# A wavelet block on one core: channel maxima turned by VectorE, sums kept as rows, and a part of the residual added by engines

## The chip, the cores and the metric

One core of one Trainium2 chip. The metric is device time in microseconds (us) of one launch, median of several runs.

## The reference

x is (8, 256, 160, 160) in float32: 8 images of 256 channels. Weights are small.

```python
wav = concat(haar_dwt(x))                      # 4*256 channels, 80 x 80
fused = relu(bn1(conv1x1(wav, fusion_w, fusion_b)))       # 256 channels
sp_in = concat([mean(fused, channels), max(fused, channels)])
spatial_out = sigmoid(conv7x7(sp_in, sa_w)) * fused
ch_map = sigmoid(mlp(mean(spatial_out, hw)) + mlp(max(spatial_out, hw)))
projected = relu(bn2(conv1x1(ch_map * spatial_out, proj_w, proj_b)))  # 4*256
return haar_idwt(projected) + x
```

So `proj` of an image can start only when the channel gates of the whole image are known, and these only when its 80 x 80 map of channel means and maxima is complete.

## The kernel before, in words

Channels lie on 128 partitions in 2 halves (`i` or `o`). An image is cut into 14 tiles of rows (`ROWS`, line 15: 6 rows of 80 pixels, or 5), so 112 tiles in all; a tile of 6 rows has 480 pixels and 1,920 values of x for each channel half. The program is software pipelined in *slots* (`Slot`, line 21): slot `k` computes `fused` of tile `k` (the *fusion*) and projects tile `kc = k - LAG`, with `LAG = 14 + EXTRA = 20`. So the first 20 slots only fuse (the fill), the next 92 do both (the main phase), and the last 20 only project (the tail). The slot's `phase` is its place in the image that follows the one whose map is being finished: phase 0 ends the convolution, phases 1 to 4 multiply the image by the gates of space in 8 chunks (`GATED`, line 214), and phase 6 (`LAST`) has the channel gates. Each engine has one program and runs it in the order written; semaphores join them.

- **TensorE** (`body`, line 415): `fusion(s, 0)`, `project(s, 0)`, `turn`, `fusion(s, 1)`, `project(s, 1)`. A fusion or a projection of one half is 24 matmuls of 128x128 weights with the tile's pixels (L389, L375; float32 as a high and a low part in three products). `turn` (L410, L412) transposes the row maxima `mx` and multiplies `sm` by ones, row by row, so that both maps lie with columns on partitions in the PSUM tile `pm`. The 7x7 convolution is 14 matmuls (L443).
- **VectorE** (`body`, line 698): `x_lower` (L615, low part of x), `butterflies` (L645, L647, PSUM and `relu` to `sd`), `cells` (L659, `sd` to the output tile), `spatial` (L693, L695, from `turn`'s PSUM to `maps`), `lower` (L676, `y_lo`), `gate` (L669), `channel_max` (L684).
- **ScalarE**: `x_upper` (L463), `relus` (L492), `upper` (L509), `fused` (L536), `chunk_means` (L501).
- **GpSimd** (POOL): `channel_sum` (L314) and `add_x` (L321), a DMA that adds x from DRAM onto the output tile in SBUF. There are 4 output buffers `xout`.
- **SyncE** (SP): the loads of x (L254), the stores (L259, which wait for `x_added`), and the round trip of the space gate through DRAM (L270, L263).

Two places of the code say what sets the order around the change:

```python
for r in range(rows):                       # turn, on TensorE
    pe.transpose(pm[0:W2, r * P:(r + 1) * P], mx[:, r * W2:(r + 1) * W2], ident[:, :])
for r in range(rows):
    mm = pe.matmul(pm[0:W2, MEANS + r:MEANS + r + 1], sm[:, r * W2:(r + 1) * W2],
                   ones[:, 0:1], start=True, stop=True)
```

## Time and profile before

| what | value |
|---|---|
| median of 3 runs | 2601.07 us (2600.91 to 2601.85) |
| the profiled execution | 2597.0 us, span 2595.1 us |
| TensorE busy | 2469.7 us, 95% |
| VectorE busy | 1994.8 us, 77% |
| ScalarE busy | 1077.9 us, 42% |
| GpSimd busy | 355.2 us, 14% |
| DMA | 659.91 MB, 254 GB/s over the span |

A page's busy time is the union of an engine's instructions. "Idle before" says how long an engine stood still ahead of a group and what ended that. An average over the whole span mixes the fill, the main phase and the tail, so the stretches have to be read apart.

### The profile page before, as it was taken

What the parts mean: (1) busy time and instruction counts of PE and PEld (TensorE: products, weight loads), DVE (VectorE), ACT (ScalarE), POOL (GpSimd) and SP (SyncE); (2) the same over time, 40 slices, a digit from 0 to 9 for tenths busy, and PEclk for the clock granted to TensorE, in tenths of its full rate; (3) what the DMA queues carried; (4) which work ended last, traced back from release to release, by engine and by line L of the source; (5) the groups of instructions that cost most, each with busy time, mean ns of one, the idle gap of its engine ahead of it and who ended that gap; (6) DMA issues with size and microseconds to landing.
All of it is one profiled execution on the core that took longest, in us unless ns stands there. A gap on an engine that the chain in (4) does not pass through costs nothing. (4 is left out here: it accounts for less than half of the span.)

```text
span 2595.1 us, 32968 instructions
## 1 busy us (share of the span) xinstructions
PE 2469.7 (95%) x12996; PEld 2200.7 (85%) x12996; DVE 1994.8 (77%) x2560; ACT 1077.9 (42%) x1413; POOL 355.2 (14%) x346
## 2 busy tenths in 40 slices
PE   4999999999999999999999999999999999987874
PEld 3888889898898989989898988989899898976764
DVE  4656777798778887798777987788877987787875
ACT  2445534354344533354434543345333453334221
POOL 0100111111111111111111111111111111111110
PEclk9999999999999999999999999999999999998897
DMA  3445699999999999999999999999999999898999
GB/s 125 157 147 195 185 267 262 257 297 270 256 270 273 287 261 260 250 304 271 265 266 256 303 263 261 262 280 286 260 259 263 295 268 267 242 248 237 277 272 245
DMA packets 115178, 659.91 MB, mean 254 GB/s; under 512 B 19520, under 2 KB 20560, under 8 KB 115024
## 3 DMA queue, kind: packets, MB, share of 16 engines
q1 hardware_dynamic: 82768, 448.07, 48.8%
q0 software_dynamic: 32256, 209.73, 41.6%
q8 instruction: 103, 1.69, 0.2%
q14 instruction: 51, 0.42, 0.0%
HBM read 447.83 MB, written 209.92 MB: 253 GB/s over the span
## 5 line engine op out<-in xcount | busy, mean ns | idle before, releaser
L375 PE MATMUL pp<-y_hi,wp_hi 128*128 128x480 f32 (+1 forms) x1792 | 674.5, 376 | 59.1 <-DVE y_lo L676 35.8
L615 DVE TENSOR_TENSOR x_lo<-xin,x_hi 128x1920 fp32r<-128x1920 f32 (+1 forms) x224 | 474.0, 2116 | 302.3 <-ACT x_hi L463 302.2
L389 PE MATMUL pf<-x_hi,wf_hi 128*128 128x480 f32 (+1 forms) x1792 | 676.4, 377 | 6.5 <-ACT fused L536 3.5
L375 PE MATMUL pp<-y_lo,wp_hi 128*128 128x480 f32 (+1 forms) x1792 | 670.6, 374 | 0.0
L375 PE MATMUL pp<-y_hi,wp_lo 128*128 128x480 f32 (+1 forms) x1792 | 669.0, 373 | 0.0
L389 PE MATMUL pf<-x_lo,wf_hi 128*128 128x480 f32 (+1 forms) x1792 | 664.5, 371 | 0.0
L389 PE MATMUL pf<-x_hi,wf_lo 128*128 128x480 f32 (+1 forms) x1792 | 664.3, 371 | 0.0
L463 ACT ACTIVATE x_hi<-xin 128x1920 fp32r<-128x1920 f32 (+1 forms) x224 | 418.5, 1869 | 572.1 <-PE pf L389 572.1
L659 DVE SCALAR_TENSOR_TENSOR xout<-sd,both 128x960 f32<-128x960 f32 (+1 forms) x448 | 504.8, 1169 | 49.2 <-DMA out_dram<-xout 41.9
L492 ACT ACTIVATE relu<-pp,t 128x480 f32<-128x480 f32 (+1 forms) x448 | 286.3, 642 | 390.4 <-PE pp L375 349.0
L375 PEld LDWEIGHTS pp<-y_hi,wp_hi 128*128 128x128 f32 x1792 | 341.9, 191 | 110.0 <-DVE y_lo L676 40.6
L321 POOL DMA_DIRECT2D xout<-in_x_dram x224 | 196.7, 878 | 1679.7 <-DVE xout L659 1679.7
L389 PEld LDWEIGHTS pf<-x_hi,wf_hi 128*128 128x128 f32 x1792 | 337.1, 188 | 51.0 <-issue 13.2
L375 PEld LDWEIGHTS pp<-y_hi,wp_lo 128*128 128x128 f32 x1792 | 341.5, 191 | 41.2
L375 PEld LDWEIGHTS pp<-y_lo,wp_hi 128*128 128x128 f32 x1792 | 341.2, 190 | 38.6
L389 PEld LDWEIGHTS pf<-x_lo,wf_hi 128*128 128x128 f32 x1792 | 336.9, 188 | 39.5
L389 PEld LDWEIGHTS pf<-x_hi,wf_lo 128*128 128x128 f32 x1792 | 337.4, 188 | 36.4
L645 DVE SCALAR_TENSOR_TENSOR sd<-pp,nbias,relu 128x480 f32<-128x480 f32 (+1 forms) x448 | 306.6, 684 | 22.2 <-PE pp L375 19.9
L536 ACT ACTIVATE fused<-pf,t 128x480 f32<-128x480 f32 (+1 forms) x224 | 141.0, 643 | 400.3 <-PE pf L389 400.2
L647 DVE SCALAR_TENSOR_TENSOR sd<-pp,nbias,relu 128x480 f32<-128x480 f32 (+1 forms) x448 | 305.7, 682 | 0.0
L314 POOL TENSOR_TENSOR sm<-fused 128x480 f32<-128x480 f32 (+1 forms) x112 | 159.4, 1423 | 545.0 <-DVE mx L684 261.5
L669 DVE CUSTOM_DVE_ANT_0 fused<-fused,sigb 128x800 f32<-128x800 f32 x128 | 121.7, 988 | 54.1 <-DMA sigb<-sig_scratch 54.1
(82 smaller groups left out, 1117.2 us busy)
## 6 DMA issues: line engine op xcount, KB each, us to landing
xin<-in_x_dram SPq DMA_DIRECT2D x160, 960.0 KB, 8.3
xout<-in_x_dram POOLq DMA_DIRECT2D x160, 960.0 KB, 10.9
out_dram<-xout SPq DMA_DIRECT2D x160, 960.0 KB, 11.8
xin<-in_x_dram SPq DMA_DIRECT2D x64, 800.0 KB, 7.5
xout<-in_x_dram POOLq DMA_DIRECT2D x64, 800.0 KB, 10.7
out_dram<-xout SPq DMA_DIRECT2D x64, 800.0 KB, 11.0
sigb<-sig_scratch SPq DMA_DIRECT2D x64, 400.0 KB, 8.1
fused<-in_L_conv_fusion_w_dram SPq DMA_DIRECT2D x1, 1024.0 KB, 4.9
```

What stands on the lines that cost most here:

```text
L314: nc.gpsimd.tensor_tensor(sm[:, 0:n], fused[:, 0, ring(s.k)], fused[:, 1, ring(s.k)], ALU.add).then_inc(sm_ready, 1)
L321: nc.gpsimd.dma_start(xout[:, g % 4, 0:4 * px_of(kc)], dram(x_v, kc, i), accum_op=ALU.add).then_inc(x_added[g % 4], 16)
L375: mm = pe.matmul(pp[j][:, 0:n_px], w[:, kt, cols], y[:, s.pc, kt, 0:n_px], start=(kt == 0 and m == 0), stop=(kt == CT - 1 and m == 2))
L389: mm = pe.matmul(pf[o][:, 0:n_px].rearrange("p (y w) -> p y w", w=W2), w[:, i, q, o * P:(o + 1) * P], v[:, q % 2, :, q // 2, :], start=(i ...
L463: nc.scalar.activation(halves(x_hi, i, k), pairs(i, k), ACT.Copy).then_inc(xhi_ready[i], 1)
L492: nc.scalar.activation(relu[:, n, 0:n_px], pp[j][:, 0:n_px], ACT.Relu, bias=bias2[:, j * CT + i:j * CT + i + 1]).then_inc(r_ready, 1)
L536: nc.scalar.activation(fused[:, o, ring(s.k)], pf[o][:, 0:px_of(s.k)], ACT.Relu, bias=bias1[:, o:o + 1]).then_inc(f_ready, 1)
L615: nc.vector.tensor_tensor(halves(x_lo, i, k), pairs(i, k), halves(x_hi, i, k).bitcast(F32), ALU.subtract).then_inc(xlo_ready[i], 1)
L645: nc.vector.scalar_tensor_tensor(rows[:, :, 0, :], p, low, q, ALU.max, ALU.add).then_inc(sd_ready, 1)
L647: nc.vector.scalar_tensor_tensor(rows[:, :, 1, :], p, low, q, ALU.max, ALU.subtract).then_inc(sd_ready, 1)
L659: nc.vector.scalar_tensor_tensor(px[:, :, :, c], s0, both[:, c, i:i + 1], s1, ALU.add, op).then_inc(cell_ready, 1)
L669: nc.vector.tensor_tensor_reduce(f, f, sigb[:, :], 1.0, 0.0, ALU.mult, ALU.max, part[:, 1, i, c:c + 1]).then_inc(mult_done, 1)
```

## The change

Five things are changed.

1. `turn` is gone. VectorE turns `mx` in blocks of 32x32 (`turn`, now on VectorE) and takes the maximum over each block into `blockmax`; once per image TensorE transposes `blockmax` (2 transposes into `across`), VectorE takes the maxima over the 4 partition groups, and SyncE sends the map through DRAM to lay it as rows. `mx` and `turned` lie in `sd`.
2. The channel sums are gathered by rows in PSUM: one matmul per row, with `pick` as weights, which puts the sum of row `at` into PSUM row `at` of a group of 32; ScalarE scales the finished map once per image.
3. `EXTRA` is 7, so `LAG` is 21; the convolution moves from phase 0 to phase 1, `GATED` to phases 2 to 5, `LAST` is 7.
4. x is added by DMA only for half `i = 1` of a tile, and only while `kc + LAG < NT` (not in the tail). Otherwise x is loaded by SyncE into `xre`, the projection's result goes to `cell`, and VectorE adds one half of the pixels and GpSimd the other (`residual`). There are 3 buffers `xre` where there were 4 `xout`.
5. GpSimd's additions wait for VectorE's `x_lower`.

```diff
-EXTRA = 6
+EXTRA = 7
-        xout = sb("xout", [P, 4, XPM])
+        xre = sb("xre", [P, 3, XPM])
-        mx = sb("mx", [P, PXM])
+        cell = sb("cell", [P, XPM])
+        mx = sd[:, 0, 0:PXM]
+        turned = sd[:, 1, 0:PXM]
-        GATED = {1: (0, 1), 2: (2, 3), 3: (4, 5), 4: (6, 7)}
+        GATED = {2: (0, 1), 3: (2, 3), 4: (4, 5), 5: (6, 7)}
+        def adding(kc, i):
+            return i == 1 and kc + LAG < NT
+        def residual(eng, ops, kc, i, hand, added):
+            g = 2 * kc + i
+            n = 2 * px_of(kc)
+            part_of = slice(hand * n, (hand + 1) * n)
+            eng.wait_ge(xre_landed[g % 3], 16 * uses(g, False))
+            eng.wait_ge(cell_ready, 2 * (g + 1))
+            x_part = xre[:, g % 3, part_of]
+            ops.tensor_tensor(x_part, x_part, cell[:, part_of], ALU.add).then_inc(added, 1)
...
             def body(s):                                   # SyncE
+                if s.phase in GATED:
+                    load_sig(s, GATED[s.phase][0])
+                if s.load_second:
+                    load_x(s.k + 2, 0)
+                if s.c and not s.c_is_first:
+                    store(s.kc - 1, 1)
+                if s.c and not adding(s.kc, 1):
+                    load_residual(s.kc, 1)
+                if s.phase in GATED:
+                    load_sig(s, GATED[s.phase][1])
+                if s.load_second:
+                    load_x(s.k + 2, 1)
+                if s.phase == 0:
+                    sp.wait_ge(maxima_ready, s.nb + 1)
+                    sp.dma_start(map_dram.rearrange("o (h p j) -> (o p) h j", h=2, j=GROUP), maxima[:, :, :]
+                                 ).then_inc(map_stored, 16)
...
+                if s.c:
+                    store(s.kc, 0)
+                if s.c_next:
+                    load_residual(s.kn, 0)
+                if s.phase == 0:
+                    sp.wait_ge(map_stored, 16 * (s.nb + 1))
+                    need(sp, conv_psum, s.nb)
+                    sp.dma_start(maps[:, 1, PAD:PAD + W2], map_dram.rearrange("o (h w) -> (o h) w", w=W2)
+                                 ).then_inc(map_landed, 16)
...
             def body(s):                                   # GpSimd
+                if s.c and not s.c_is_first:
+                    if adding(s.kc - 1, 1):
+                        add_x(s.kc - 1, 1)
+                    else:
+                        residual(gp, nc.gpsimd, s.kc - 1, 1, 1, added_p)
+                if s.turn:
+                    channel_sum(s)
                 if s.c:
-                    add_x(s.kc, 1)
+                    if s.load_next:
+                        gp.wait_ge(xlo_ready[1], s.k + 2)
+                    elif s.c_next and not s.next_is_first:
+                        gp.wait_ge(lo_ready, CT * (s.kn + 1))
+                    residual(gp, nc.gpsimd, s.kc, 0, 1, added_p)
...
+            def add_channels(s):                           # TensorE
+                k = s.k - 1
+                pe.wait_ge(sm_ready, k + 1)
+                for r in range(ROWS[k % TILES]):
+                    row = FIRST[k % TILES] + r
+                    at, base = row % GROUP, row - row % GROUP
+                    m = min(GROUP, H2 - base)
+                    mm = pe.matmul(sums[base:base + m, :], pick[:, GROUP - 1 - at:GROUP - 1 - at + m],
+                                   sm[:, r * W2:(r + 1) * W2], start=(at == 0), stop=(at == m - 1))
...
+                if s.phase == 1:
+                    pe.wait_ge(mean_ready, s.nb + 1)
+                    pe.wait_ge(map_landed, 16 * (s.nb + 1))
...
+            def turn(s):                                   # VectorE
+                nc.vector.transpose(turned[:, 0:blocks * GROUP], mx[:, 0:blocks * GROUP]).then_inc(turned_ready, 1)
+                nc.vector.tensor_reduce(blockmax[:, block:block + blocks],
+                                        turned[:, 0:blocks * GROUP].rearrange("p (n c) -> p n c", c=GROUP),
+                                        AX.X, ALU.max).then_inc(blockmax_ready, 1)
...
                 if s.c:
                     butterflies(s, 1)
+                    residual(dve, nc.vector, s.kc, 0, 0, added_v)
                     cells(s, 1)
```

**Three places of the order.** TensorE around a turn of the second image, before: L375 is the end of `project(s, 0)`, L410 and L412 are `turn`, L389 begins `fusion(s, 1)`.

```order
L375 MATMUL pp<-y_hi,wp_hi 128x480
L375 MATMUL pp<-y_hi,wp_lo 128x480
L375 MATMUL pp<-y_lo,wp_hi 128x480
L410 MATMUL pm<-ident,mx 80x128 x6
L412 MATMUL pm<-ones,sm 80x1 x6
L389 MATMUL pf<-x_hi,wf_hi 128x480
```

With the change, in phase 1 of the same image: L467 is the end of `fusion(s, 1)`, L486 is `add_channels`, L517 the convolution, L453 begins `project(s, 1)`.

```order
L467 MATMUL pf<-x_hi,wf_hi 128x480
L467 MATMUL pf<-x_hi,wf_lo 128x480
L467 MATMUL pf<-x_lo,wf_hi 128x480
L486 MATMUL pm<-sm,pick 32x80 x6
L517 MATMUL pm<-maps,band 80x80 x14
L453 MATMUL pp<-y_hi,wp_hi 128x480
```

The six transposes of a slot are gone, the six sums have 80 moving columns where they had one, they stand behind both fusions, and the convolution stands in the slot of phase 1 where it closed that of phase 0.

VectorE in a slot of the main phase with the change (L733 and L735 are the butterflies, L753 the cells, L786 the channel maximum, L698 `x_lower`):

```order
L770 SCALAR_TENSOR_TENSOR y_lo<-fused,ch,y_hi 128x480 x2
L786 TENSOR_TENSOR sd<-fused 128x480
L698 TENSOR_TENSOR x_lo<-xin,x_hi 128x1920
L795 STREAM_TRANSPOSE sd<-sd 128x480
L798 TENSOR_REDUCE blockmax<-sd 128x15
L733 SCALAR_TENSOR_TENSOR sd<-pp,nbias,relu 128x6x80
```

The transpose and the reduction stand between `x_lower` and the second butterflies; `spatial`'s two instructions, which stood ahead of `y_lo`, are gone.

SyncE around the end of an image with the change (L296 loads x, L304 loads the residual, L313 stores):

```order
L296 DMA xin<-in_x_dram 128x1920
L337 DMA map_scratch<-maxima 100x2x32
L313 DMA out_dram<-xre 128x1920
L304 DMA xre<-in_x_dram 128x1920
L351 DMA maps<-map_scratch 80x80
L296 DMA xin<-in_x_dram 128x1920
L313 DMA out_dram<-xre 128x1920
L296 DMA xin<-in_x_dram 128x1920
L342 DMA sig_scratch<-sig 80x80
```

The rows of L337 and L351 are new: a store and a load of the map of maxima, with one store and one load of a tile between them.

## Rows read from the trace of the kernel before

**Rows 1.** Windows: main phase, tail to LAST, rest of tail; busy by engine, PEclk, DMA share.
```profile
330.00:2200.00 1870.00, 1870.00 (x9959) 1676.89 (x9958) 1502.86 (x1848) 816.24 (x1070) 277.94 (x258) 1.00 0.97 270
...
2283.40:2379.50 96.10, 69.82 (x322) 59.34 (x320) 78.29 (x119) 36.51 (x70) 11.01 (x13) 0.88 0.98 261
2379.50:2595.10 215.60, 155.36 (x672) 132.63 (x672) 149.04 (x196) 51.43 (x84) 24.72 (x29) 0.88 0.97 255
```

**Rows 2.** Line 516, ScalarE's gate of space, in two successive images.
```profile
L516 ACT ACTIVATE sig<-pm x1: 234/234/234, 784.8 to 784.8; 80x80 f32<-80x80 f32 x1
...
L516 ACT ACTIVATE sig<-pm x1: 234/234/234, 1088.6 to 1088.6; 80x80 f32<-80x80 f32 x1
```

**Rows 3.** Timeline of PE around one turn: start us, us, engine, line.
```profile
641.68 0.38 PE L375 MATMUL pp<-y_hi,wp_lo 128*128 128x480 f32 x1
...
642.77 0.82 PE L410 MATMUL pm<-ident,mx 128*80 128x128 f32 x6
643.42 0.95 PE L412 MATMUL pm<-ones,sm 128*80 128x1 f32 x12
644.24 0.46 PE L389 MATMUL pf<-x_hi,wf_hi 128*128 128x480 f32 x1
644.54 0.38 PE L389 MATMUL pf<-x_hi,wf_lo 128*128 128x480 f32 x1
```

**Rows 4.** Timeline of PE around one convolution.
```profile
478.78 2.17 PE L443 MATMUL pm<-band,maps 80*80 80x80 f32 x28
480.74 0.46 PE L389 MATMUL pf<-x_hi,wf_hi 128*128 128x480 f32 x1
```

**Rows 5.** Timeline of DVE, a slot without gates.
```profile
641.82 0.71 DVE L645 SCALAR_TENSOR_TENSOR sd<-pp,nbias,relu 128x480 f32<-128x480 f32 x1
...
644.44 2.35 DVE L659 SCALAR_TENSOR_TENSOR xout<-sd,both 128x960 f32<-128x960 f32 x2
646.71 0.94 DVE L693 TENSOR_REDUCE maps<-pm 80x6 f32<-80x768 f32 x1
...
647.64 1.33 DVE L676 SCALAR_TENSOR_TENSOR y_lo<-fused,ch,y_hi 128x480 fp32r<-128x480 f32 x2
```

**Rows 6.** Timeline of DVE, slots with gates.
```profile
499.24 0.99 DVE L669 CUSTOM_DVE_ANT_0 fused<-fused,sigb 128x800 f32<-128x800 f32 x1 [1.72 <-DMA sigb<-sig_scratch]
...
501.07 0.66 DVE L684 TENSOR_TENSOR mx<-fused 128x480 f32<-128x480 f32 x1
501.64 2.15 DVE L615 TENSOR_TENSOR x_lo<-xin,x_hi 128x1920 fp32r<-128x1920 f32 x1
...
523.90 3.13 DVE L615 TENSOR_TENSOR x_lo<-xin,x_hi 128x1920 fp32r<-128x1920 f32 x1 [0.24 <-ACT x_hi L463]
```

**Rows 7.** Timeline of POOL in the same slots.
```profile
501.87 3.01 POOL L314 TENSOR_TENSOR sm<-fused 128x480 f32<-128x480 f32 x1 [5.28 <-issue]
...
523.79 1.22 POOL L314 TENSOR_TENSOR sm<-fused 128x480 f32<-128x480 f32 x1 [3.49 <-issue]
```

**Rows 8.** The page, DMA queues (packets, MB, share) and issues (KB, us to landing).
```profile
q1 hardware_dynamic: 82768, 448.07, 48.8%
q0 software_dynamic: 32256, 209.73, 41.6%
...
sigb<-sig_scratch SPq DMA_DIRECT2D x64, 400.0 KB, 8.1
...
sig_scratch<-sig SPq DMA_DIRECT2D x8, 25.0 KB, 13.0
```

**Rows 9.** Timeline of DVE in the tail.
```profile
2385.51 0.72 DVE L645 SCALAR_TENSOR_TENSOR sd<-pp,nbias,relu 128x480 f32<-128x480 f32 x1 [4.62 <-PE pp L375]
...
2403.03 1.34 DVE L676 SCALAR_TENSOR_TENSOR y_lo<-fused,ch,y_hi 128x480 fp32r<-128x480 f32 x2
...
2414.28 1.34 DVE L676 SCALAR_TENSOR_TENSOR y_lo<-fused,ch,y_hi 128x480 fp32r<-128x480 f32 x2
```

**Rows 10.** Waits of DVE in the tail: us in total, times, longest.
```profile
DVE xout L659 <- DMA out_dram<-xout: 41.9, 20, 4.9
```

More of the change, by code:

```diff
@@ L289, in _ @@
                 body(s)
-            for i in range(CT):
-                store(NT - 1, i)
-            for p in range(4):
-                sp.wait_ge(stored[p], 16 * len(range(p, 2 * NT, 4)))
+            store(NT - 1, 1)
+            for p in range(3):
+                sp.wait_ge(stored[p], 16 * len(range(p, 2 * NT, 3)))
         @block.gpsimd
@@ L429, in body @@
-                if s.c:
+                elif s.c:
                     pe.wait_ge(lo_ready, CT * (s.kc + 1))
                     project(s, 0)
-                if s.phase != LAST:
-                    if s.turn:
-                        turn(s)
-                    if s.a:
-                        fusion(s, 1)
+                if s.a:
+                    fusion(s, 1)
+                if s.turn:
+                    add_channels(s)
+                if s.phase == 0:
+                    pe.wait_ge(blockmax_ready, s.k)
+                    for h in range(2):
+                        n = NPX // GROUP // 2
+                        mm = pe.transpose(across[:, h * P:(h + 1) * P], blockmax[:, h * n:(h + 1) * n], ident[:, :])
+                    mm.then_inc(across_psum, 1)
@@ new lines, in body @@
+                if s.phase == 1:
+                    pe.wait_ge(mean_ready, s.nb + 1)
+                    pe.wait_ge(map_landed, 16 * (s.nb + 1))
+                    pe.wait_ge(band_pass, KS * NK)
+                    for j in range(NK):
+                        mm = pe.matmul(conv, band[:, j, :], maps[:, j // KS, j % KS:j % KS + W2],
+                                       start=(j == 0), stop=(j == NK - 1))
+                    mm.then_inc(conv_psum, 1)
+                if s.phase == LAST:
+                    pe.wait_ge(lo_ready, CT * (s.kc + 1))
+                    project(s, 0)
@@ L533, in body @@
                 if s.a:
+                    if s.phase == LAST and s.c:
+                        act.wait_ge(lo_ready, CT * (s.kc + 1))
                     for o in range(CT):
@@ L636, in butterflies @@
                 n_px = px_of(s.kc)
+                if s.a and (i == 1 or s.phase == LAST):
+                    dve.wait_ge(turned_ready, s.k + 1)
+                    dve.wait_ge(blockmax_ready, s.k + 1)
                 for n, j in enumerate((LL, HL)):
@@ L707, in body @@
                     lower(s.kc)
-                if s.c and not ahead:
+                elif s.c:
                     butterflies(s, 0)
+                    if not s.c_is_first and not adding(s.kc - 1, 1):
+                        residual(dve, nc.vector, s.kc - 1, 1, 0, added_v)
                     cells(s, 0)
-                if s.turn and not ahead:
-                    spatial(s)
                 if s.c_next and not s.next_is_first and not ahead:
@@ L719, in body @@
                     nc.vector.tensor_reduce(pool[:, :, 1], part[:, 1, :, :], AX.X, ALU.max).then_inc(pool_ready, 1)
-                if ahead and s.turn:
-                    spatial(s)
                 if s.phase in GATED:
@@ L727, in body @@
                     x_lower(s.k + 1, 1)
+                if s.a:
+                    turn(s)
+                if s.phase == 0:
+                    spatial_max(s)
                 if ahead:
```

207 lines of the change are left out of this document (112 added, 95 removed).

## The prediction

> **What bounds the kernel now.** I read the windows first, by stage. In the main phase (330 to 2200 us) TensorE is busy for all of 1870.00 us at a granted clock of 1.00, VectorE for 1502.86 us (80%), and the DMA engines for 0.97 of the time [rows 1]. The reader should see that nothing there ever stops TensorE; whatever shortens its own work shortens the main phase, and nothing else does. The period confirms it: the space gate of one image stands at 784.8 us and that of the next at 1088.6 [rows 2], 303.8 us apart. The tail is another matter. From its start at 2283.4 to the y_lo of LAST it takes 96.1 us, and from there to the end, for 14 tiles, 215.6 us; TensorE is busy in only 72% of either part at a mean clock of 0.88, while the DMA share stays at 0.97 to 0.98 [rows 1]. VectorE waits there 20 times, 41.9 us in all, for a store to free an output buffer [rows 10]. So the tail is bound by transfers: per byte the DMA that adds costs 41.6/209.73, against 48.8/448.07 for plain ones, 1.8 times as much [rows 8].
>
> **The change, part by part**, against the profiled execution's 2597.0 us.
>
> *TensorE's map work.* Before, one turn of six rows goes from 642.77 to 644.24, 1.47 us, and the first matmul behind it takes 0.30 us to the next one instead of 0.22 (642.77 less 641.68 is five steps of 0.218) [rows 3]: 1.55 us. Five rows by the same rates: 1.31. With the change a row is one float32 matmul of 80 moving columns. Its nearest row is the convolution, 14 matmuls in 1.96 us [rows 4], so 0.14 us each; six make 0.84, with the same 0.08 behind them 0.92 us, five 0.78. Saved: 0.63 and 0.53 us. An image has ten tiles of six rows and four of five, 8.4 us, and eight images 67 us. The new `across` transposes, 2 a image at the old transposes' 0.11 and 0.08 behind them, cost 0.3 us, 2 us in all. **-65 us.** Bounds: 0.11 us a row (the transposes, 0.65/6 [rows 3]) and 0.245 (a whole row of the old turn, 1.47/6) give -84 and 0. I take the convolution's price since shape and type agree.
>
> *VectorE in the main phase.* Gone: the reduction and scaling, from 646.71 to 647.64, 0.93 us [rows 5]. New in a slot of six rows: the addition of 960 elements, half an x_lower of 1920 (2.15 us [rows 6]), 1.07; a transpose of 480 elements and a reduction to 15 columns. Neither is in the trace. For each I take the step of the channel maximum over the same 480 elements, 0.57 us (501.07 to 501.64 [rows 6]); bounds are half of that and the old reduction's 0.94 [rows 5]. Net +1.28 us a slot. VectorE's busy time per image is 1502.86/1870 of 303.8, 244 us, and becomes about 261 of 295: 88%. The fullest slots are those with gates: two x_lower 4.3, eight butterflies 5.2 (four from 641.82 to 644.44), four cells 4.5 (two from 644.44 to 646.71 [rows 5]), y_lo 1.3, maximum 0.57, four gate halves 3.7 (two from 499.24 to 501.07 [rows 6]), and the new 2.2: 21.8 us. TensorE's slot is 96 steps of 0.218 and 0.92, 21.9 us. That fits by a hair, between slots with 3.7 us to spare. I cost it at nothing: TensorE covers it, and if that cover is gone each us of excess is a us of the slot.
>
> *The map's round trip.* In phase 0 VectorE's maxima over the groups come behind its transpose and reduction, by the order of the program about 22 us into the slot; the convolution stands some 17 us into the next slot of 22, 17 us later. Between lie a small store, whose like takes 13.0 us to land, and a small load, with 8.1 us for the load of the gates [rows 8]: 21.1 and some 0.7 us of issue, against 17. With half of the adding DMAs gone the engines' share falls from 0.97 to about 0.86 (the software queue's 41.6% of engine time halves, and plain loads take up 0.55 of that half), so I take 18.9 us in place of 21.8: a wait of 2 us in each of the 7 images of the main phase, **+15 us**. Bounds: 0 and 5 us each, 0 and 35. Behind SyncE's wait for the first of these stand the second and then the next slot's x; x of that slot waits for an x_lower that is not done earlier anyway. What is late next is the gate load of phase 2, a slot later than before, so it has the same room as now.
>
> *The longer lag.* One slot of the main phase becomes a slot of the fill: 48 steps of 0.218 less, **-10.5 us**; the tail gets it back below.
>
> *The tail.* The adding DMAs go, and a tile needs 3.93 MB of plain transfer. At 448.07 MB in 48.8% of 2595 us (354 GB/s [rows 8]) that is 11.1 us, and TensorE's 48 steps are 10.5. VectorE takes over: with no wait it went from one y_lo at 2403.03 to the next at 2414.28 in 11.25 us [rows 9], and two additions of 1.07 make 13.4 (11.2 with five rows). From LAST's y_lo to the end: 6 us until the first butterflies (to 2385.51 [rows 9]), ten tiles of 13.4 and four of 11.2 for 179 us, and 9 us for the last addition (GpSimd's 960 elements twice its 1.22 [rows 7]) and a store of 6 us: 194, against 215.6, -22 us. Ahead of LAST there are now seven slots for six: two of 13.4, a stall of 6 for the map's round trip, which nothing covers there, three of 13.4 + 3.7 + 0.5 with gates, one such of five rows 15.4, and 14.2 for the last: 115 against 96.1, +19 us. **-3 us.** Bounds: the present 215.6/14 = 15.4 us a tile gives +22 instead of -22 in the second part, a wait-free TensorE's 10.5 gives -50.
>
> *Everything else* goes together at 0: 2 small copies by ScalarE per image, the loads at the start, the convolution's own 14 matmuls.
>
> Sum: 2597.0 - 65 + 15 - 10.5 - 3 = 2533.5 us. The runs' median, 2601.07, lies 4.1 us above the profiled 2597.0, so I forecast **2538 us**, 2.4% less.
>
> **GpSimd beside VectorE.** The trace shows that these two hinder each other. GpSimd's sum that began at 501.87, while VectorE was in the x_lower of 501.64, took 3.01 us instead of 1.22, and the x_lower that began at 523.90, 0.11 us after GpSimd's sum, took 3.13 instead of 2.15 [rows 6, 7]. Each lost about what was left of the other's instruction. The change adds GpSimd 960 elements a slot, 2.4 us, twice that in the tail, but makes it wait for x_lower, behind which VectorE has a transpose, a reduction and butterflies with one operand in PSUM. In the main phase that is 0.57 + 0.57 + 2.6 = 3.7 us of cover for 2.4 us, so the sum has nothing for it. The Trainium skill (SBUF — State Buffer, "Who interferes with whom") says that a VectorE instruction with two SBUF inputs and a GpSimd instruction that reads SBUF take one shared port, that whichever starts first keeps it for its whole length, and that one with a single SBUF input is free of it. By that rule the trace agrees, and the sum stands as long as the two stay apart; where they meet, its time is the last rival's.
>
> **The rivals.**
>
> *The round trip holds TensorE up.* If both transfers take as long as now or longer (queued behind a tile's store and load, about 9 us of wait), 7 x 9 replaces 15: 2586 us. For: 13.0 and 8.1 are the rows. Against: less DMA work.
>
> *The tail stays bound by transfers.* Three buffers for four, each held for a load, an addition and a store; if a tile takes 15.4 us as now, the second part costs 216 in place of 194 and the first some 10 more: 2570 us. For: a share of 0.97. Against: 11.1 us of transfer per 13.4.
>
> *Better than forecast.* The sums cost 0.11 us a row, the map arrives in time, the additions run beside waits: 2538 - 17 - 15 = 2506 us.
>
> *Slower than before: GpSimd meets VectorE.* Place: the main phase, where GpSimd has 1.2 + 2.4 us a slot. If these fall on two-input instructions, VectorE's gated slots take 21.8 + 3.6 = 25.4 against 21.9: 3.5 us for four slots of an image, 7 images, 98 us, so 2538 + 98 = 2636 us. It decides once more than 2.3 us of the 3.6 fall so in every gated slot. Against: the new waits, with 3.7 us of cover. For: VectorE has no time to spare there.
>
> **How the numbers follow.** Forecast 0.50, round trip 0.14, tail 0.13, better 0.14, GpSimd 0.09. The time is the forecast's. The range takes in the better case, the tail and the round trip with the forecast's own bounds, 2503 to 2594, and leaves out GpSimd's case and the ends. A measurement of this kernel can tell about 0.2%, 5 us, from no change. Only the last case is slower; between it and the others little is left: faster 0.88, same 0.03, slower 0.09.
>
> **What would show it.** TensorE 100% busy in the main phase with images 296 us apart plus the wait; a turn of six sums near 0.92 us; a wait of TensorE on the map's DMA near 2 us once an image; VectorE near 88%; additions of 960 at 1.07 us on VectorE and 2.4 on GpSimd; tail tiles of 13.4 us with VectorE without waits. The forecast is wrong if TensorE waits for VectorE in the gated slots, if x_lower or cells get longer on average, or if VectorE waits for stores or for `xre` in the tail.

## The result, and the profile after

| | before | changed |
|---|---|---|
| median | 2600.99 us | 2618.7 us (2616.93 to 2620.59, 4 runs) |
| profiled execution, span | 2597.0, 2595.1 us | 2619.5, 2617.7 us |
| ratio to before | | 1.0072, 95% interval 1.0054 to 1.0089 |

The change makes the kernel 0.7% slower. I forecast 2538 us in 2503 to 2594, so the time is outside the range and its sign is wrong. The channel gates (ScalarE's sigmoid into `ch`, line 524 before and 596 now) cut a run into comparable stretches; the same table serves for the experiments.

| stretch | before | changed | difference |
|---|---|---|---|
| start to the first channel gates | 291.4 | 299.4 | +8.0 |
| six images of the main phase, each | 303.8 | 307.2 | +3.4, six times +20.5 |
| the last image to its gates | 264.3 | 279.3 | +15.0 |
| from there to the end | 216.5 | 195.6 | -20.9 |

The transfers changed as intended. The adding DMAs are down from 209.73 MB at 41.6% of engine time to two fifths of that [rows 8]:

```profile
q1 hardware_dynamic: 104368, 573.01, 61.2%
q0 software_dynamic: 13104, 85.20, 16.8%
...
xin<-in_x_dram SPq DMA_DIRECT2D x160, 960.0 KB, 6.4
...
xre<-in_x_dram POOLq DMA_DIRECT2D x65, 960.0 KB, 11.4
...
sigb<-sig_scratch SPq DMA_DIRECT2D x64, 400.0 KB, 5.3
```

The gates' own load lands in 5.3 us at the median where it took 8.1. But that median mixes two: in 330 to 2200 us the first gate's load of a slot takes 10.1 us at the median, where it took 8.6, and the second one's 4.7, where it took 8.2. The windows of [rows 1] now read:

```profile
core 0: us, PE busy (x) PEld busy (x) DVE busy (x) ACT busy (x) POOL busy (x), PEclk, DMA share, GB/s
330.00:2200.00 1870.00, 1831.62 (x9390) 1607.09 (x9390) 1596.13 (x1922) 812.18 (x1070) 362.39 (x255) 0.99 0.85 268
2283.40:2379.50 96.10, 70.34 (x294) 57.72 (x292) 83.11 (x99) 27.49 (x49) 26.32 (x11) 0.83 0.69 234
2379.50:2595.10 215.60, 167.59 (x724) 141.71 (x725) 202.41 (x258) 63.08 (x108) 65.58 (x30) 0.92 0.74 262
```

The first row is where the kernel loses. TensorE, never idle there before, now stands still for 1870.00 - 1831.62 = 38.4 us, though VectorE is busy for only 1596.13 us, 85%. Who stops TensorE, in the waits of the same window:

```profile
PE pm L486 <- POOL sm L384: 23.0, 13, 2.9
PE pp L453 <- DVE sd L735: 14.0, 10, 2.4
```

Two releasers: GpSimd's channel sum (`sm`) and VectorE's butterflies (`sd`). Neither is the map's round trip, which costs nothing in this window. The wait for `sd` goes back to a VectorE that is late in slots with gates. Of the 23.0 us for `sm`, six waits of 2.9 us lie elsewhere, in the slot of the channel gates. VectorE's timeline from the first gate of one slot (gate A; its second is gate B) to gate A of the next slot:

```profile
860.74 0.99 DVE L763 CUSTOM_DVE_ANT_0 fused<-fused,sigb 128x800 f32<-128x800 f32 x1 [2.70 <-DMA sigb<-sig_scratch]
...
864.87 0.67 DVE L795 STREAM_TRANSPOSE sd<-sd 128x480 f32<-128x480 f32 x1
865.58 0.65 DVE L798 TENSOR_REDUCE blockmax<-sd 128x15 f32<-128x480 f32 x1
866.32 0.72 DVE L733 SCALAR_TENSOR_TENSOR sd<-pp,nbias,relu 128x480 f32<-128x480 f32 x1
...
868.83 1.15 DVE L271 TENSOR_TENSOR xre<-xre,cell 128x960 f32<-128x960 f32 x1
...
872.16 0.98 DVE L763 CUSTOM_DVE_ANT_0 fused<-fused,sigb 128x800 f32<-128x800 f32 x1
...
873.98 1.82 DVE L698 TENSOR_TENSOR x_lo<-xin,x_hi 128x1600 fp32r<-128x1600 f32 x1
...
884.59 0.99 DVE L763 CUSTOM_DVE_ANT_0 fused<-fused,sigb 128x800 f32<-128x800 f32 x1 [3.48 <-DMA sigb<-sig_scratch]
```

From 860.74 to 884.59 are 23.85 us, of which VectorE waits 3.48 for `sigb`. In between it has no other gap, so its work is 20.4 us, in a slot that is partly of tiles of five rows; in the fullest slots, with six rows throughout, it is 22.0, for the 21.8 of the prediction. The work is as the sum said, and it is the wait ahead of the gate that doesn't fit. That wait isn't new: in 330 to 2200 us VectorE waited as long in all for these loads before, in shorter pieces (first line before, second changed; total, times, longest):

```profile
DVE fused L669 <- DMA sigb<-sig_scratch: 40.6, 31, 2.4
DVE fused L763 <- DMA sigb<-sig_scratch: 41.3, 19, 3.5
```

New are the longer single waits and a slot without slack to take them up. The reader should find the cause in SyncE's queue and GpSimd's timeline of that slot:

```profile
870.01 0.34 SPq L313 DMA_DIRECT2D out_dram<-xre  x1
870.39 0.43 SPq L304 DMA_DIRECT2D xre<-in_x_dram  x1
874.09 0.32 SPq L319 DMA_DIRECT2D sigb<-sig_scratch  x1
```

```profile
865.04 2.27 POOL L271 TENSOR_TENSOR xre<-xre,cell 128x960 f32<-128x960 f32 x1 [11.61 <-DVE x_lo L698]
872.60 0.88 POOL L391 DMA_DIRECT2D xre<-in_x_dram  x1 [5.29 <-DVE xre L753]
875.95 1.19 POOL L384 TENSOR_TENSOR sm<-fused 128x480 f32<-128x480 f32 x1 [2.47 <-issue]
```

The gate's load is issued at 874.09, once the gate before it is done with the one buffer, behind a store of 960 KB (870.01), the new load of x (870.39, 800 KB) and the adding DMA (872.60). It lands at 884.6, in 10.5 us. And the sum of 875.95 begins when VectorE's x_lower (873.98, behind gate B) is over, because the change makes it wait for that: point 5 of the change names this wait for the additions alone, but the channel sum has it too (`xlo_ready[0]`), where it waited for `mx_ready` before. TensorE then stands still:

```profile
877.18 1.02 PE L486 MATMUL pm<-sm,pick 128*32 128x80 f32 x12 [1.53 <-POOL sm L384]
...
891.19 0.46 PE L453 MATMUL pp<-y_hi,wp_hi 128*128 128x400 f32 x1 [2.40 <-DVE sd L735]
892.05 0.54 PE L453 MATMUL pp<-y_hi,wp_lo 128*128 128x400 f32 x1
...
901.82 0.34 PE L453 MATMUL pp<-y_hi,wp_hi 128*128 128x400 f32 x1
...
920.35 0.88 PE L486 MATMUL pm<-sm,pick 128*32 128x80 f32 x10 [2.92 <-POOL sm L384]
```

The longest wait, 2.92 us, is in the slot of the channel gates. Behind the wait of 2.40 us the same matmul takes 0.54 instead of 0.34 us until 895.05: the granted clock is at 1.2 GHz for 3.4 us (0.51 in 891.9 to 895.3). Ten steps of 0.33 us instead of 0.18 cost another 1.5.

The turn itself, in the layout of [rows 3]:

```profile
948.43 0.38 PE L467 MATMUL pf<-x_lo,wf_hi 128*128 128x480 f32 x1
948.74 1.02 PE L486 MATMUL pm<-sm,pick 128*32 128x80 f32 x12
949.68 0.48 PE L453 MATMUL pp<-y_hi,wp_hi 128*128 128x480 f32 x1
950.00 0.38 PE L453 MATMUL pp<-y_hi,wp_lo 128*128 128x480 f32 x1
```

From 948.43 to 950.00 are 1.57 us, two steps of 0.218 of which are the fusion's and the projection's own: 1.13 us for six rows, where I had 0.92. The saving is 0.42 us a turn, not 0.63.

In the tail, VectorE and GpSimd ahead of the last channel gates, and TensorE's convolution:

```profile
2334.29 0.99 DVE L763 CUSTOM_DVE_ANT_0 fused<-fused,sigb 128x800 f32<-128x800 f32 x1
...
2335.20 3.01 DVE L763 CUSTOM_DVE_ANT_0 fused<-fused,sigb 128x800 f32<-128x800 f32 x1
...
2338.14 0.70 DVE L733 SCALAR_TENSOR_TENSOR sd<-pp,nbias,relu 128x480 f32<-128x480 f32 x1
```

```profile
2334.45 2.90 POOL L271 TENSOR_TENSOR xre<-xre,cell 128x960 f32<-128x960 f32 x1 [5.15 <-DVE y_lo L770]
```

```profile
2310.97 4.00 PE L517 MATMUL pm<-maps,band 80*80 80x80 f32 x28 [8.12 <-issue]
```

GpSimd's addition starts 0.16 us into the first gate half and takes 2.90 us instead of 2.27, and the second half takes 3.01 us instead of 0.99. That happens in each of the eight gates of this stretch, twice with 2.7, in all 15.5 us. The convolution waits 8.12 us for the map, once, where nothing covers it.

### The profile page after: what moved, and what is told of

Same layout as the page of the kernel before. It is cut to its first block and busy times, and to the rows that moved or that the text cites. A ratio compares the mean times of both kernels' runs of the same rounds, so it can differ in the third digit from the quotient of the medians.

```text
span 2617.7 us, 32607 instructions
## 1 busy us (share of the span) xinstructions
PE 2445.5 (93%) x12372; PEld 2135.2 (82%) x12372; DVE 2180.0 (83%) x2701; ACT 1078.3 (41%) x1421; POOL 513.5 (20%) x347
## 5 line engine op out<-in xcount | busy, mean ns | idle before, releaser
L453 PE MATMUL pp<-y_hi,wp_hi 128*128 128x480 f32 (+1 forms) x1792 | 691.1, 386 | 78.3 <-DVE sd L735 44.7
L453 PE MATMUL pp<-y_lo,wp_hi 128*128 128x480 f32 (+1 forms) x1792 | 675.9, 377 | 0.0
L453 PE MATMUL pp<-y_hi,wp_lo 128*128 128x480 f32 (+1 forms) x1792 | 674.7, 377 | 0.0
L467 PE MATMUL pf<-x_hi,wf_hi 128*128 128x480 f32 (+1 forms) x1792 | 668.4, 373 | 3.8 <-DVE x_lo L698 3.0
L467 PE MATMUL pf<-x_hi,wf_lo 128*128 128x480 f32 (+1 forms) x1792 | 665.3, 371 | 0.0
L467 PE MATMUL pf<-x_lo,wf_hi 128*128 128x480 f32 (+1 forms) x1792 | 664.9, 371 | 0.0
L698 DVE TENSOR_TENSOR x_lo<-xin,x_hi 128x1920 fp32r<-128x1920 f32 (+1 forms) x224 | 461.7, 2062 | 221.6 <-ACT x_hi L539 221.6
L271 POOL TENSOR_TENSOR xre<-xre,cell 128x960 f32<-128x960 f32 (+1 forms) x133 | 297.0, 2233 | 1124.7 <-DVE x_lo L698 806.9
L453 PEld LDWEIGHTS pp<-y_hi,wp_hi 128*128 128x128 f32 x1792 | 345.4, 193 | 143.4 <-DVE sd L735 57.0
L453 PEld LDWEIGHTS pp<-y_hi,wp_lo 128*128 128x128 f32 x1792 | 345.7, 193 | 38.8
L453 PEld LDWEIGHTS pp<-y_lo,wp_hi 128*128 128x128 f32 x1792 | 345.1, 193 | 39.1
L467 PEld LDWEIGHTS pf<-x_hi,wf_hi 128*128 128x128 f32 x1792 | 337.0, 188 | 47.2 <-issue 5.6
L467 PEld LDWEIGHTS pf<-x_hi,wf_lo 128*128 128x128 f32 x1792 | 337.7, 188 | 39.0
L467 PEld LDWEIGHTS pf<-x_lo,wf_hi 128*128 128x128 f32 x1792 | 337.1, 188 | 39.1
L733 DVE SCALAR_TENSOR_TENSOR sd<-pp,nbias,relu 128x480 f32<-128x480 f32 (+1 forms) x448 | 307.9, 687 | 38.2 <-PE pp L453 27.7
L753 DVE SCALAR_TENSOR_TENSOR cell<-sd,both 128x960 f32<-128x960 f32 (+1 forms) x266 | 299.8, 1169 | 9.4 <-POOL xre L271 2.2
L735 DVE SCALAR_TENSOR_TENSOR sd<-pp,nbias,relu 128x480 f32<-128x480 f32 (+1 forms) x448 | 306.4, 684 | 0.0
L384 POOL TENSOR_TENSOR sm<-fused 128x480 f32<-128x480 f32 (+1 forms) x112 | 134.9, 1205 | 486.3 <-DVE x_lo L698 277.5
L753 DVE SCALAR_TENSOR_TENSOR xre<-sd,both 128x960 f32<-128x960 f32 (+1 forms) x182 | 204.6, 1166 | 0.0
```

What stands on the lines that cost most here:

```text
L271: ops.tensor_tensor(x_part, x_part, cell[:, part_of], ALU.add).then_inc(added, 1)
L384: nc.gpsimd.tensor_tensor(sm[:, 0:n], fused[:, 0, ring(k)], fused[:, 1, ring(k)], ALU.add).then_inc(sm_ready, 1)
L453: mm = pe.matmul(pp[j][:, 0:n_px], w[:, kt, cols], y[:, s.pc, kt, 0:n_px], start=(kt == 0 and m == 0), stop=(kt == CT - 1 and m == 2))
L467: mm = pe.matmul(pf[o][:, 0:n_px].rearrange("p (y w) -> p y w", w=W2), w[:, i, q, o * P:(o + 1) * P], v[:, q % 2, :, q // 2, :], start=(i ...
L698: nc.vector.tensor_tensor(halves(x_lo, i, k), pairs(i, k), halves(x_hi, i, k).bitcast(F32), ALU.subtract).then_inc(xlo_ready[i], 1)
L733: nc.vector.scalar_tensor_tensor(rows[:, :, 0, :], p, low, q, ALU.max, ALU.add).then_inc(sd_ready, 1)
```

## The experiments

Three explanations stood after the result. Waits: VectorE is late in the gated slots since the gates' load stands behind the added transfers, and the channel sum stands behind a late x_lower. Contention: GpSimd's additions take VectorE's time. Map: TensorE's part of the change is itself no gain. Twelve kernels were run; an expectation's letters A and B hold for its own run. The stretches in the table come from the profiled executions. The kernel before had medians of 2599.0 to 2599.6 us beside these runs, single ones between 2585 and 2607, so a few us between two rows of the table say nothing unless one stretch holds them. How much a stretch itself varies is seen in e6, e7, e8 and e10, which run the same program until the tail: their images last 302.5, 301.5, 302.1 and 302.8 us, so differences of 1 us an image between rows are not told apart.

| run | median us | ratio, 95% interval | to first gates | each of six images | last image | to the end |
|---|---|---|---|---|---|---|
| before | 2601 | 1 | 291.4 | 303.8 | 264.3 | 216.5 |
| changed | 2618.7 | 1.0072 (1.0054 to 1.0089) | 299.4 | 307.2 | 279.3 | 195.6 |
| e1_all_dma | 2600.6 | 1.0014 (0.9997 to 1.0031) | 300.6 | 302.2 | 262.8 | 220.2 |
| e2_dma_main | 2580.5 | 0.9940 (0.9919 to 0.9961) | 299.9 | 302.4 | 268.4 | 195.5 |
| e3_sum_free | 2625.9 | 1.0120 (1.0085 to 1.0155) | 289.9 | 309.7 | 278.8 | 196.2 |
| e4_sig_first | 2601.8 | 1.0015 (1.0000 to 1.0029) | 300.1 | 304.2 | 278.5 | 196.1 |
| e5_sum_last | 2608.4 | 1.0038 (1.0024 to 1.0051) | 290.8 | 307.0 | 278.6 | 196.3 |
| e6_dma_sum | 2571.3 | 0.9895 (0.9865 to 0.9925) | 290.0 | 302.5 | 269.7 | 195.2 |
| e7_dma_tail | 2559.0 | 0.9857 (0.9826 to 0.9888) | 289.8 | 301.5 | 261.0 | 195.5 |
| e8_quarter | 2567.2 | 0.9882 (0.9852 to 0.9912) | 290.8 | 302.1 | 262.2 | 201.4 |
| e9_two_causes | 2588.1 | 0.9949 (0.9933 to 0.9966) | 289.7 | 303.7 | 278.4 | 196.1 |
| e10_vector_all | 2586.2 | 0.9948 (0.9934 to 0.9963) | 291.1 | 302.8 | 261.8 | 220.2 |
| e11_sums_twice | 2628.9 | 1.0106 (1.0091 to 1.0121) | 303.7 | 310.0 | 265.9 | 194.7 |
| e12_best | 2562.1 | 0.9846 (0.9831 to 0.9861) | 291.1 | 302.2 | 261.0 | 195.6 |

**e1_all_dma.** The map's part of the change alone, with three buffers. Here, in e2 and in all kernels built on them the queue's order in SyncE changes as well, beside the line shown: the store of half 0 comes a slot later, and the store and the load of x for half 1 stand behind the second gate's load:

```diff
-            return i == 1 and kc + LAG < NT
+            return True
```

> The map part of the change alone: x is added by DMA for every half tile, in the tail too; VectorE and GpSimd add nothing. Theory A (VectorE is overfull in the four gated slots, 22.1 us of work and 3 us of waiting for the gates against TensorE's 21.9): without the additions VectorE has 1.1 us less per slot, TensorE's waits of 6.4 us an image go, images are about 299.5 us apart, and the tail is bound by transfers as before, so 2575 to 2600 us. Theory B (GpSimd's channel sum, which now waits for x_lower, is what stops TensorE): that wait is still there, TensorE still waits some 6 us an image, images near 306 us, about 2615 us.

It lies between the two: TensorE's wait for `sd` in 330 to 2200 us falls from 14.0 to 3.5 us, as in A, and 13.4 of the 23.0 us for `sm` stay, as in B. An image lasts 302.2 us, 1.6 less than before where the prediction's turns and `across` gave 8, and the start is 9 us slower. The tail behind the last gates is no shorter than before. So the map's part gains little as it stands, and x by engines in the tail is worth 25 us, from 220.2 to 195.6. Ahead of the last gates it costs: all 16 gate halves of e1's tail take 0.99 us, and from the last gate of space (ScalarE's `sig`) to the last channel gates are 91.2 us, where the changed kernel takes 107.1. The difference, 15.9 us, is that kernel's 15.5 us of slow gates.

**e2_dma_main.** x by DMA for both halves in the main phase, by engines in the tail:

```diff
-            return i == 1 and kc + LAG < NT
+            return kc + LAG < NT
```

> x is added by DMA for both halves outside the tail, by the engines in the tail. Theory A: images 299.5 us apart instead of 307.2, tail as in the changed kernel (195.6 us behind LAST), so 2619 less 7 times 7.7, about 2565 us. Theory B: images near 306 us, about 2610 us. If the two adding DMAs bind again (a share near 0.97), the x loads or stores show up as waits.

2580.5 us, between A and B, and faster than both kernels, by 38 us than the changed one. An image lasts 302.4 us where it lasted 307.2, so the engines' additions in the main phase are what costs there: 4.8 us an image, in spite of a DMA share of 0.96 instead of 0.85 in 330 to 2200 us. It doesn't tell waits from contention: both the loads of `xre` and the additions are gone. The last image gains 11 us too, though the engines add there as before. In its tail only four gate halves are slow (7.7 us) where eight were; the load of x for half 1 now comes later in the queue, but whether that is why wasn't tried.

**e3_sum_free.** The channel sum no longer waits for x_lower:

```diff
-                if s.load_next:
-                    gp.wait_ge(xlo_ready[0], s.k + 2)
```

> GpSimd's channel sum no longer waits for x_lower of the slot, only for fused and for its own PSUM group. Theory B: TensorE's waits on sm (about 4 us an image) go and nothing comes for them, about 2590 us. Theory A: TensorE then waits for VectorE's sd instead, and GpSimd now meets two-input instructions of VectorE, 2605 to 2620 us.

It is slower than theory A's 2620, and shows what that wait buys. The gates on VectorE in 330 to 2200 us, of the changed kernel and of this one:

```profile
L763 DVE CUSTOM_DVE_ANT_0 fused<-fused,sigb 128x800 f32<-128x800 f32 x96 | 91.2, 988 | 41.3 <-DMA sigb<-sig_scratch 41.3
```

```profile
L761 DVE CUSTOM_DVE_ANT_0 fused<-fused,sigb 128x800 f32<-128x800 f32 x96 | 126.2, 1351 | 12.8 <-DMA sigb<-sig_scratch 12.8
```

The mean gate half goes from 988 to 1351 ns, 35 us more work, of which 28.5 are won back as shorter waits for `sigb`; an image lasts 2.5 us longer. But the start is 9.5 us shorter (289.9 for 299.4): where nothing is projected, the wait buys nothing and holds TensorE up 17 times for 0.4 to 1.5 us, 11.8 us in all. That gave e5.

**e4_sig_first.** SyncE issues the next slot's first gate load before the load of x into `xre`:

```diff
                 if s.c:
                     store(s.kc, 0)
+                if s.phase is not None and s.phase + 1 in GATED:
+                    load_sig(s, GATED[s.phase + 1][0])
                 if s.c_next:
                     load_residual(s.kn, 0)
```

> SyncE issues the first gate load of a slot ahead of the load of the residual instead of behind it. Theory A: VectorE's waits for the gates (41 us in the main phase) fall by about half, TensorE's waits with them, 3 us an image, about 2597 us. Theory B: VectorE waits less, TensorE as long as before, 2619 us.

17 us less, near theory A's 2597, with all the additions and bytes in place. The waits of TensorE and, in the second fence, of VectorE in 330 to 2200 us:

```profile
PE pm L486 <- POOL sm L384: 21.0, 12, 2.9
PE pm L528 <- DVE pool L833: 1.7, 6, 0.3
```

```profile
DVE fused L763 <- DMA sigb<-sig_scratch: 8.3, 10, 2.3
```

VectorE's wait for `sigb` falls from 41.3 to 8.3 us, and TensorE's wait for `sd`, 14.0 us before, is gone. The first gate's load now lands in 7.8 us at the median (10.1), the second one's in 6.4 (4.7). That shows the explanation by waits: a queue's order made VectorE late, in slots that its work already fills (e12 tries the same order where it has slack). It gives 3.0 of the 4.8 us an image that e2 gave. The wait for `sm`, 2.9 us in the slot of the channel gates, is untouched.

**e5_sum_last.** The sum waits only where it buys something:

```diff
-                if s.load_next:
+                if s.load_next and s.c and s.phase != LAST:
                     gp.wait_ge(xlo_ready[0], s.k + 2)
```

> The changed kernel, but GpSimd's channel sum waits for the next tile's low halves only in slots that also project and are not the slot of the channel gates; in the first 17 slots and in that one slot of each image it starts as soon as the tile's fused values stand. Theory A (the sum's wait, put there so that it runs beside no VectorE work it would slow, is itself a price: 0.7 us of TensorE in each of the first 17 slots and 2.9 us once an image, with a clock dip behind it): the first channel gates come at 290 instead of 299.4, an image lasts 307.2 less 3 to 4 us, in all 2618.7 - 9.5 - 7 x 3.5 = 2585. Theory B (as when the wait was dropped everywhere, the sum then runs beside VectorE's work and slows it, so that nothing is won in the main phase): the first 9.5 us alone, 2609, or worse.

Theory B's 2609 is met: 10 us, nearly all at the start. In the main phase it gives 0.2 us an image, less than can be told apart. In the slot of the channel gates the sum starts earlier but meets x_lower and y_lo on VectorE and takes 1.95 us where it took 1.37 (906.61 here, 918.93 before), so TensorE still waits 2.3 us for it, for 2.9.

**e6_dma_sum.** e2 and e5 together.

> x by DMA for both halves of each tile in the main phase, engines in the tail, and the channel sum's wait dropped as in the run before. With VectorE unloaded the sum can start early without harm. Theory A: 290 for the first channel gates, an image of 302.4 less 2.2 us of wait less 1.5 us of clock = 299, 268 for the last interval, 195.5 behind it: 2550. Theory B (302.4 an image is what TensorE's work and clock make of it, the sum's wait only stands where another wait would): 290 first, 302.4 an image: 2571.

2571.3, theory B's number; that it fits to the microsecond is luck, its four runs lie between 2566 and 2571.5. The start takes 290.0 us, an image 302.5. TensorE's idle time in 330 to 2200 us didn't fall (17.4 us in e2, 20.1 here): the waits for `sm` got shorter and waits for VectorE came in their place.

**e7_dma_tail.** As e6, with x by DMA up to the last image but one:

```diff
-            return kc + LAG < NT
+            return kc + TILES < NT
```

> As the run before, with x by DMA also for the tiles of the second but last image that are finished in the tail, so that the gates there have no GpSimd work beside them; the engines add x for the last image alone. Theory A (the second gate of each of these slots took 3.0 instead of 1.0 us beside GpSimd's addition, which makes the last interval 268 where it is 263 with x by DMA): 5 us less than the run before. Theory B (that stretch is held by the map's round trip and the butterflies' chain, or with the DMA engines full again it pays what it gains): within 2 us of it.

12 us less than e6, of which 8.7 in the stretch that it changes, more than theory A's 5; the rest lies in images whose program is the same. In e6 four gate halves of that stretch were slow, 7.7 us in all; here none is. A second gate half there, of e2 and of this kernel:

```profile
2322.56 3.01 DVE L769 CUSTOM_DVE_ANT_0 fused<-fused,sigb 128x800 f32<-128x800 f32 x1
```

```profile
2306.17 0.99 DVE L769 CUSTOM_DVE_ANT_0 fused<-fused,sigb 128x800 f32<-128x800 f32 x1
```

So contention is real, and its place is the tail's gates. At 0.9857 of the time before this is, with e12, the fastest version found.

**e8_quarter.** As e7, VectorE adds a quarter of each half tile, GpSimd three quarters:

```diff
-            part_of = slice(hand * n, (hand + 1) * n)
+            part_of = slice(0, 1 * n // 2) if hand == 0 else slice(1 * n // 2, 2 * n)
```

> As the run before, but VectorE adds x to a quarter of each half tile and GpSimd to three quarters (each had a half), for the last image's 14 tiles, behind the last channel gates. That stretch is 195.5 us with VectorE busy 93 per cent. Theory A (VectorE's own work bounds it): each tile saves two times 0.57 us on VectorE, 14 x 1.15 = 16 us less than the run before. Theory B (while GpSimd reads and writes, VectorE's operations of the same kind stand still or nearly so, as y_lo's did, 3.34 against 1.33 us): GpSimd's two additions last 4.5 instead of 3.0 us each and VectorE loses up to that much again: no gain, or up to 20 us slower.

Theory B: the last stretch is 201.4 for 195.5. VectorE's and GpSimd's addition in one half tile:

```profile
2463.95 1.21 DVE L271 TENSOR_TENSOR xre<-xre,cell 128x400 f32<-128x400 f32 x1
```

```profile
2461.94 2.77 POOL L271 TENSOR_TENSOR xre<-xre,cell 128x1200 f32<-128x1200 f32 x1 [3.88 <-DVE y_lo L776]
```

GpSimd's ends at 2464.71, 0.76 us into VectorE's, which takes 1.21 us for half the elements of what took 0.98 in e7: it stands until the other is through, then works 0.45. Four of these additions, with 0.28, 0.63, 0.75 and 0.76 us beside GpSimd's, all end 0.43 to 0.45 us behind it. With a half, GpSimd's 1.92 us end within the four butterflies.

**e10_vector_all.** As e7, VectorE adds all of it in the last image:

```diff
+            if hand:
+                return
...
-            part_of = slice(hand * n, (hand + 1) * n)
+            part_of = slice(0, 2 * n)
```

> As the kernel with x by DMA up to the second but last image (2559), but VectorE adds x to the whole of each half tile and GpSimd to none of it, for the last image's 14 tiles; that stretch is 195.5 us, with VectorE busy 93 per cent. Theory A (VectorE's own work bounds it, and GpSimd's half is a gift): VectorE has two times 1 us more in each tile, 14 x 2 = 28 us slower, 2587. Theory B (GpSimd's half costs VectorE nearly as much as it takes away, as the run with three quarters on GpSimd suggests): under 10 us slower, 2559 to 2569.

Theory A here: 27 us slower, 24.7 of them in that stretch, against 28 expected. GpSimd's half is nearly free where it lies beside butterflies, and a half is the best of the three shares tried.

**e9_two_causes.** The changed kernel with the edits of e4 and e5:

> The changed kernel with both of its causes of lateness taken out that were tried apart: the first gate's load goes ahead of the x load in its queue (alone 17 us), and the channel sum waits for the low halves only in slots that project and are not the channel gates' (alone 10 us). Theory A (two separate causes; the second gained only 1 us in the main phase since the first still stood behind it): 2618.7 - 17 - 10 = 2592, and 2585 if the second now gains in the main phase too, with images of about 302.5. Theory B (they overlap: both paid for the same late VectorE): 2600.

2588.1, faster than before, where e4 and e5 alone give 17 and 10 of the 30.6 us: two causes that add, and a little more, at theory A's figures for the time but not for its images of 302.5. An image lasts 303.7, still 2 more than in e7, and the traces show where. In the slot of the channel gates VectorE's addition of 0.98 us stands ahead of its cells, GpSimd's adding DMA waits for the cells, and the channel sum comes behind it. TensorE around 900 us, in e9 and in e7:

```profile
899.58 1.23 PE L486 MATMUL pm<-sm,pick 128*32 128x80 f32 x10 [2.31 <-POOL sm L384]
```

```profile
895.88 0.88 PE L492 MATMUL pm<-sm,pick 128*32 128x80 f32 x10 [1.51 <-POOL sm L388]
```

The wait is 0.8 us longer, and beside it the granted clock is at 1.2 GHz for 3.4 us in each of e9's six images but in only one of e7's. No run takes this wait away by itself.

**e11_sums_twice.** As e7, each row's sum matmul issued twice:

```diff
+                    for again in range(2):
```

> As the kernel with x by DMA up to the second but last image (2559), but TensorE makes each row's sum matmul twice into the same PSUM rows (the scale behind it is halved, so the result is the same). It prices the turn: a six-row turn now holds TensorE 1.13 us, of which 12 matmuls are 0.95 between their starts. Theory A (TensorE bounds fill and main phase, so what is added to its work is added to the time): 98 tiles in the fill and the main phase that fuse under TensorE's bound, and 14 more, by about 0.9 us each, 2559 + 90 to 100 = 2650 to 2660. Theory B (other engines hold the main phase, TensorE has room): under 50 us more.

Between both: 70 us more, 0.62 a tile. A six-row turn is now 1.77 us between starts, for 0.94:

```profile
1001.78 1.85 PE L493 MATMUL pm<-sm,pick 128*32 128x80 f32 x24
1003.55 0.49 PE L459 MATMUL pp<-y_hi,wp_hi 128*128 128x480 f32 x1
```

So each added row costs 0.14 us, and an image gets some 11.1 us of work (ten turns of 0.83 and four of 0.7) but lasts only 8.5 longer. TensorE is busy for 1768.06 of 1770.00 us from 330 to 2100, where it was busy for 1757.12 in e7: of the missing 2.6 us, 1.9 went into idle time that it filled. TensorE bounds both kernels, with little idle time between.

**e12_best.** e7 with the edit of e4:

> As the kernel with x by DMA up to the second but last image (2559), with the first gate's load ahead of the other loads in the queue as well. In that kernel VectorE waits only some 2.5 us an image for gates and is behind nowhere but around the channel gates. Theory A (a late gate costs only where VectorE has no slack): no gain in the main phase, 1 to 5 us in the last image's gates, 2554 to 2559. Theory B (each microsecond of a gate's wait reaches TensorE): 15 us less, 2544.

No gain, at theory A's edge: the median is 3 us above e7's, and the runs are the same, 2557.03 to 2562.52 us against e7's 2557.07 to 2565.23. A late gate costs only where VectorE has no slack.

## Why the prediction was wrong

My sum is 2533.5, a span of 2531.6; the span came out at 2617.7, 86 us more. By stretches: the terms make an image 303.8 - 8.4 + 0.3 + 2 = 297.7 us, and six images miss by 9.5 each, 57 us; the last stretch misses by 1; 28 us lie at the start and in the last image up to its gates.

- **VectorE in the main phase: the step that failed.** It said that the gated slots' 21.8 us "fits by a hair", and "I cost it at nothing: TensorE covers it". The work was as counted, 22.0 us in the fullest slots: additions of 1.15 (I had 1.07), transpose and reduction in steps of 0.71 and 0.74 (I had 0.57), GpSimd's addition 2.27 (2.4). What the list of the slot's instructions left out is that the gate itself waits for a load. The rows of before show that wait (1.72 us at 499.24 [rows 6]) and VectorE's slack hid it there; the change takes the slack away and puts a load of x in the gate load's way, which makes single waits up to 3.5 us. A slot that "fits by a hair" can't carry that wait: TensorE waited 14.0 us for VectorE's `sd` in the main phase, in place of nothing. e4 shows it: 3.0 us an image, 17 in all. I named SyncE's queue only for the map, and called the gate load "the same room as now".
- **GpSimd's channel sum: left out.** The prediction counted GpSimd's new wait for x_lower as protection and looked only at what it keeps apart. It didn't say who waits for the sum: TensorE. That costs 9 us in the fill (e5). In the main phase TensorE waits for the sum above all once an image, 2.9 us in the slot of the channel gates, and dropping the wait there takes only 0.6 us off it.
- **TensorE's map work: right mechanism, wrong size.** 1.13 us a turn instead of 0.92; a turn of six rows saves 0.42 instead of 0.63, and 112 turns by 0.21 make 24 us, the largest single miss. The rate per row was right (e11: 0.14 us). What I missed is the switch: the first one starts 0.31 us behind the last fusion step instead of 0.22 and the six then take 0.94, not 0.84. My bounds held it.
- **The map's round trip: too dear in the main phase.** I put 2 us into each of seven images (14, entered as 15). It costs none there. The maxima stand 17 us ahead of the convolution, as I had it, but the trip from the store's issue to the load's landing takes 11.8 us (771.55 to 783.3), not 18.9, and the map lies there 3.8 to 5.3 us early in six images:

```profile
771.55 0.32 SPq L337 DMA_DIRECT2D map_scratch<-maxima  x1
776.04 0.85 SPq L351 DMA_DIRECT2D maps<-map_scratch  x1
788.21 2.23 PE L517 MATMUL pm<-maps,band 80*80 80x80 f32 x28
```

  In the tail it costs 8.1 us, where I had 6.
- **The tail's second part: right.** 194.6 us for 194 from LAST's y_lo (2423.05), tiles of 13.5 us (2435.49 to 2448.99) for 13.4, no wait for transfers, -21 for -22:

```profile
2435.49 1.34 DVE L770 SCALAR_TENSOR_TENSOR y_lo<-fused,ch,y_hi 128x480 fp32r<-128x480 f32 x2
2448.99 1.34 DVE L770 SCALAR_TENSOR_TENSOR y_lo<-fused,ch,y_hi 128x480 fp32r<-128x480 f32 x2
```

- **The tail ahead of the last channel gates: too little.** The rule that I quoted from the Trainium skill (SBUF — State Buffer, "Who interferes with whom") was applied to the main phase alone. The eight gates of the tail run beside GpSimd's additions and lose 15.5 us. e1, without additions, has none of it, 91.2 us for 107.1 between the last gate of space and the last channel gates; e7 gains 8.7 in that stretch, where e6 still had 7.7 of slow gates. The trace agrees with the rule in both directions: the gate half, with two SBUF inputs, takes 3.01 for 0.99 us; transposes, reductions and butterflies beside the addition of 865.04 take the 0.67, 0.65 and 0.72 us that they take alone (0.671, 0.654 and 0.712 on average in e7).

How far does that reach? The main phase's 57 us are six times 9.5: 2.9 for the turns (14 x 0.21), less the 2 forecast for the round trip, and about 8.6 for TensorE's waits and the clock beside them. These can be read: 38.4 us of idle time and 20.5 us at 1.2 GHz in 330 to 2200 make 6.3 and some 1.5 us an image. Of the 8.6, e9 takes back 3.5 (307.2 to 303.7) and x by DMA 5.7 (e7, 301.5; 4.4 to 5.7 over the four kernels with that main phase). So the lateness has its causes in the gates' load and the engines' additions; contention shows little in the main phase, where the 96 gate halves take 0.988 us on average, as before. The rest between e9 and e7 is read from the traces as the sum's wait behind VectorE's addition, and no run shows it alone. The other 28 us: 9 for the sum at the start, 15.5 for the gates and 2 for the map in the tail, which leaves 1 or 2 for some 25 turns of 0.21 there, so the account closes only to some 4 us. Nor is e7's image explained to the end: 303.8 less 5.5 for the turns (0.42 and, with five rows, 0.32), plus 0.3 for `across` and 2.2 of idle time, makes 300.8, and it lasts 301.5, which is within what images of one program differ by.

The rivals: the one that ended slower had the right place, the gated slots, and the right sign. Its price, GpSimd's instructions falling on VectorE's, is not what happened in the main phase: VectorE's x_lower took 2157 ns on average against 2212 before. The engines there were kept apart, and the queue and the waits that kept them apart were the cost. The round trip didn't hold TensorE up, and the tail's tiles were not bound by transfers.

## What to carry to other kernels

Where an engine's slot is full to a per cent, its own work is the wrong question: list what each of its instructions waits for, and what the change puts ahead of that in a queue. A wait added to keep two engines apart has a price as well: ask who waits for the instruction behind it, stretch by stretch, since it can pay in one (the projecting slots, e3) and only cost in another (the fill, e5). A median over loads of one kind can hide that the ones that matter got slower. And an engine's addition beside a DMA's can be right in a stretch that is bound by transfers (the tail, 21 us) and wrong in one that TensorE bounds with the DMA engines hidden (the main phase, 4.8 us an image).

## What was not expected of the hardware

- A small load (400 KB) issued behind transfers of 800 and 960 KB took 10.5 us to land, and the first gate's loads 10.1 at the median, against 4.7 for the second's, of the same size. Issued ahead of one of these transfers (e4) they took 7.8. That came with the DMA share down from 0.97 to 0.85.
- VectorE's addition of two SBUF tiles, met by GpSimd's, doesn't slow in proportion but stands until the other ends: 400 elements in 1.21 us, 0.76 of it beside GpSimd, and 0.43 to 0.45 us behind its end in four cases. The instructions with an operand in PSUM keep their time beside it.
- Behind a wait of 2.40 us on TensorE the granted clock was at 1.2 GHz for 3.4 us, which adds 1.5 us to the wait. The longer one of 2.92 us at 920.35 had none behind it (1.00 in 921 to 925), so the length of the wait alone doesn't say.
